# Eight of 24 attention batches: heads in two halves of the array, a new order of beats, four homes for the stacks

## The reference, cut to what matters

```python
q = (x @ Wq + bq).reshape(B, N, 16, 8)
k = (y @ Wk + bk).reshape(B, M, 16, 8)
v = (y @ Wv + bv).reshape(B, M, 16, 8)
attn = softmax(einsum('bnhd,bmhd->bhnm', q, k) / sqrt(8))
out = einsum('bhnm,bmhd->bnhd', attn, v)
h = relu(out @ W1 + b1) @ W2 + b2
```

## Time and profile before

| what | value |
|---|---|
| median of 3 runs | 785.37 us (782.15 to 787.21) |
| profiled execution, first to last instruction | 779.4 us |
| PE busy | 638.1 us (82%), 4712 matmuls |
| DVE busy | 490.8 us (63%) |
| ACT busy | 386.3 us (50%) |
| POOL busy | 302.9 us (39%) |
| stack DMAs from `qk_parts` | 168, of 128 KB each |

### The profile page before, as it was taken

One profiled execution on the slowest core, in us unless ns is written; L12 is line 12 of the kernel. 1 busy time (PEld: TensorE's weight loads), 2 busy tenths in 40 slices (PEclk: granted clock), 3 DMA queues, 4 the chain that ended last, 5 costly groups with the idle time before them and its releaser, 6 DMA issues.

```text
span 779.4 us, 15312 instructions
## 1 busy us (share of the span) xinstructions
PE 638.1 (82%) x4712; PEld 467.2 (60%) x4712; DVE 490.8 (63%) x1428; ACT 386.3 (50%) x860; POOL 302.9 (39%) x456
## 2 busy tenths in 40 slices
PE   2688788889999887899977777748898777699997
PEld 1355666556665544899944555437796566456665
DVE  4678666877778753556867785636657665455443
ACT  5356465466666565466624655335776444232221
POOL 4435355443333036162747644372545730000000
PEclk9999999999999999699976998777999999699999
DMA  6263423333333200144354441012455100223331
GB/s 185 60 158 97 112 73 90 90 94 88 90 95 89 78 19 38 53 130 119 103 138 114 120 128 42 16 41 83 126 143 157 51 11 1 70 69 105 98 95 56
DMA packets 93575, 68.71 MB, mean 88 GB/s; under 512 B 9800, under 2 KB 84424, under 8 KB 93272
## 3 DMA queue, kind: packets, MB, share of 16 engines
q1 hardware_dynamic: 89400, 59.34, 27.4%
q0 software_dynamic: 4096, 8.40, 3.5%
HBM read 30.94 MB, written 14.35 MB: 58 GB/s over the span
## 4 chain that ended last, share of the span: by engine, by line
PE 36%; DVE 8%; issue 6%; DMA 4%; POOL 3%; ACT 3%; SPq 1%; ACTq 0%; DVEq 0%; POOLq 0%
PE ps L2396 7%; PE ps L2406 4%; PE ps L2434 4%; PE ps L2436 4%; PE ps L2447 4%; DVE negmax L975 2%; DMA late<-outputs_moe,placed 2%; PE ps L2111 1%; PE ps L2095 1%; PE ps L2035 1%; PE ps L2390 1%; PE ps L2083 1%; PE ps L2289 1%; POOL gathered L1600 1%; DVE x_sb L1295 1%
## 5 line engine op out<-in xcount | busy, mean ns | idle before, releaser
L975 DVE TENSOR_REDUCE negmax<-ps 128x2 f32<-128x512 f32 x256 | 169.7, 686 | 87.5 <-PE ps L2083 86.8
L1743 ACT ACTIVATE exps<-ps 128x512 f32<-128x512 f32 x256 | 148.6, 598 | 100.7 <-PE ps L2095 99.9
L2083 PE MATMUL ps<-stack 96*128 96x256 bf16 x512 | 102.8, 295 | 26.7 <-DVE negmax L975 23.4
L2095 PE MATMUL ps<-stack 99*128 99x256 bf16 x512 | 100.8, 287 | 19.2 <-DMA stack<-maxt 17.7
L1600 POOL DMA_INDIRECT gathered<-z,placed x64 | 62.4, 975 | 63.3 <-PE ps L2390 28.6
L1618 POOL DMA_INDIRECT late<-outputs_moe,placed x64 | 62.1, 971 | 50.8 <-issue 15.8
L2095 PEld LDWEIGHTS ps<-stack 99*128 99x128 bf16 x512 | 44.2, 102 | 60.2 <-DMA stack<-maxt 24.4
L2083 PEld LDWEIGHTS ps<-stack 96*128 96x128 bf16 x512 | 47.9, 103 | 51.5 <-DVE negmax L975 39.4
L2111 PE MATMUL ps<-exps,values 128*32 128x256 f32 x1024 | 71.9, 398 | 1.3 <-ACT exps L1743 1.0
L1984 ACT ACTIVATE gated<-ps 128x512 f32<-128x512 f32 x36 | 21.5, 597 | 83.1 <-PE ps L2436 83.1
L2406 PE MATMUL ps<-pack_moe,ht 128*128 x368 | 60.1, 288 | 1.3 <-ACT ht L1970 0.8
(11 more groups left out here) (225 smaller groups left out, 1257.4 us busy)
## 6 DMA issues: line engine op xcount, KB each, us to landing
stack<-qk_parts SPq DMA_DIRECT2D x168, 128.0 KB
stack<-weights_t SPq DMA_DIRECT2D x32, 256.0 KB, 3.3
outputs_moe<-y_kept SPq DMA_DIRECT2D x92, 64.0 KB
ht<-gathered SPq DMA_DIRECT2D x44, 128.0 KB, 2.2
pack_moe<-in_moe SPq DMA_DIRECT2D x11, 256.5 KB, 3.9
pack_moe<-in_moe SPq DMA_DIRECT2D x6, 429.5 KB, 4.1
gathered<-y_kept SPq DMA_DIRECT2D x10, 256.0 KB, 3.6
pack_moe<-in_moe SPq DMA_DIRECT2D x1, 1732.0 KB, 7.4
```

The source lines that it names most:

```text
L975: dve.tensor_reduce(negmax_of[b % 2][:, :, h:h + 1].rearrange("p t h -> p (t h)"), ps[:, h % 2, :].rearrange("p (t k) -> p t k", t=2), AX, ...
L1743: nc.scalar.activation(exps[:, i, :], ps[:, 2 + h % 2, :], ACT.Exp, scale=scale)\
L2083: last = pe.matmul(ps[:, h % 2, t * T:(t + 1) * T], st[0:MAXROW, h, 0, t * P:(t + 1) * P], st[0:MAXROW, h, 1, :], start=True, stop=True)
L2095: last = pe.matmul(ps[:, 2 + h % 2, t * T:(t + 1) * T], st[0:MAXROW + 3, h, 1, t * P:(t + 1) * P], st[0:MAXROW + 3, h, 0, :], start=True, ...
```

## The change

`att1` keeps 6 of the 9 pairs, which makes 48 partitions a head (51 with the maxima). Even heads lie in partitions 0 to 50, odd heads in 64 to 114, two heads beside each other at one place of the free axis, so that a batch takes 8 places of a stack tile. The free halves of the three tiles give four homes (`home`). In a beat in which both a column and a row of `att1` are due, one head is even and the other odd, and their four matmuls are issued alternately (`rows_beside_columns`). Columns begin in beat 8 instead of 6, averages are issued in two halves in beats 4j+14 and 4j+15, and the chain, the values, the bias, the mixing and `moe1`'s preparation get other beats. A tail step without work of a batch has 16 beats now. SP issues two DMAs for each pair (one for each half) and two for the maxima; the maxima of the batch that is about to have its columns go between the first pair and the others. The POOL memsets of padding are gone; ACT writes ones instead.

```diff
-    "att1": [(0, 0), (0, 1), (1, 0), (1, 1), (0, 2), (2, 0), (1, 2), (2, 1), (2, 2)],
+    "att1": [(0, 0), (0, 1), (1, 0), (1, 1), (0, 2), (2, 0)],
-MAXROW = 96
+MAXROW = {"att0": 96, "att1": 48, "att2": 96}
+HALF = P // 2
+HALVES = {"att0": 1, "att1": 2, "att2": 1}
-    "moe1": {"stats": ((-1, 3), (2, 3)), "rstd": ((-1, 4), (2, 4)), "norm": ((-1, 8), (2, 6)),
-             "turn": ((-1, 10), (-1, 12), (2, 13), (2, 15)), "turned": ((-1, 11), (-1, 13), (3, 0), (3, 1)),
-             "logits": (-1, 15), "top": (0, 1), "pick": (0, 4), "mark": (0, 6), "exp": (0, 7), "rank": (0, 8),
-             "place": (0, 9), "weigh": (1, 12), "load": (2, 6), "logits2": (3, 3)},
+    "moe1": {"stats": ((-1, 11), (2, 11)), "rstd": ((-1, 12), (2, 12)), "norm": ((-1, 14), (2, 15)),
+             "turn": ((-1, 15), (0, 2), (3, 2), (3, 3)), "turned": ((0, 0), (0, 3), (3, 3), (3, 4)),
+             "logits": (0, 5), "top": (0, 6), "pick": (0, 7), "mark": (0, 9), "exp": (0, 10), "rank": (0, 11),
+             "place": (0, 12), "weigh": (1, 12), "load": (2, 6), "logits2": (3, 6)},
-SEND_FROM = {"moe1": 12, "moe2": 7}
+SEND_FROM = {"moe1": 14, "moe2": 7}
-COL_BEAT = {8: 3, 16: 6}
-GROUP_LAG = 5
-VALUE_BEAT = 4
+COL_BEAT = {8: 3, 16: 8}
+GROUP_LAG = {8: 5, 16: 6}
+GROUP_BEATS = {8: 1, 16: 2}
+VALUE_BEAT = {8: 4, 16: 12}
-PLACE_BEAT = {8: 5, 16: 7}
-MIX_BEATS = {"stats": (5, 5), "rstd": (6, 6), "norm": (7, 10), "turn": (3, 5), "turned": (4, 6), "rk": (6, 10), "gate": (7, 11),
-             "gated": (5, 6), "mixed": (6, 7)}
-CHAIN = ("turn", "finish", "turn_o", "ot", "proj", "hid", "proj2", "residual")
-CHAIN_BEATS = {8: (1, 2, 4, 5, 6, None, None, 7), 16: (1, 2, 4, 5, 6, 7, 9, 10)}
+PLACE_BEAT = {8: 5, 16: 13}
+ROOT_BEAT = {8: 0, 16: 4}
+BIAS_BEAT = {8: 3, 16: 11}
+HOMES = 4
+MIX_BEATS = {"stats": (5, 5), "rstd": (6, 6), "norm": (7, 10), "turn": (3, 7), "turned": (4, 8), "rk": (6, 10), "gate": (7, 11),
+             "gated": (5, 9), "mixed": (6, 10)}
+CHAIN = ("turn", "finish", "turn_o", "ot", "proj", "proj_b", "hid", "proj2", "proj2_b", "residual")
+CHAIN_BEATS = {8: (1, 2, 4, 5, 6, None, None, None, None, 7), 16: (1, 2, 5, 5, 8, 9, 10, 12, 13, 14)}
...
+        def home(s, b):
+            if s == "att1":
+                return 3 + b % HOMES, stack[min(b % HOMES, 2)], 8 * (b % HOMES < 3)
+            return buf(s, b), stack[buf(s, b)], 0
...
-                heads = max([H[s] for s, b in (m, a, d) if valid(b)], default=8)
+                heads = max([H[s] for s, b in (m, a, d) if valid(b)], default=H[stages[-1]] if g > last else 8)
...
+            def spread_slot(s, p, j):
+                nh, dh, (i, st, first), n = H[s], D // H[s], home(s, p), len(SLOTS[s])
+                qa, kc = SLOTS[s][j]
+                for half in range(HALVES[s]):
+                    at = half * HALF + j
+                    sp.dma_start(st[at:at + n * (dh - 1) + 1:n, first:first + nh // HALVES[s], :, :],
+                                 qk_parts[half::HALVES[s], qa:3 + kc + 1:3 + kc - qa, :]).then_inc(stack_in[i], 16)
...
+                    if spreads and sm == "att1":
+                        spread_first(s, p)
+                    if valid(a):
+                        place_maxima(sa, a)
+                    if spreads:
+                        spread_rest(s, p) if sm == "att1" else spread_heads(s, p)
...
-            def fill_rows(i):
-                rows = stack[i][64:MAXROW, 8:16, :, :].rearrange("p h a t -> p (h a t)").bitcast(F32)
-                nc.scalar.activation(rows, zt[64:MAXROW, 0, 0:1].to_broadcast([MAXROW - 64, 8 * T]), ACT.Copy)\
-                    .then_inc(rows_filled, 1)
+            def fill_rows(p):
+                if p == HOMES - 1:
+                    wait(act, "cols_psum", "att0", B - 1)
+                _, st, first = home("att1", p)
+                write_ones(slice(32, HALF), st, first)
+                write_ones(slice(32 + HALF, P), st, first).then_inc(rows_filled, 1)
+                if (s, p, u) == ("att1", 2, 10):
+                    fill_rows(HOMES - 1)
+                    if j == 5:
+                        wait(act, "cols_psum", "att1", B - 1)
+                        fill_ones(2)
...
+            def row_half(s, m, h, t):
+                (at, k), (_, st, first) = half_place(s, h), home(s, m)
+                st = st[at:at + MAXROW[s], first + k, :, :]
+                return pe.matmul(ps[:, h % 2, t * T:(t + 1) * T], st[:, 0, t * P:(t + 1) * P], st[:, 1, :], start=True, stop=True)
+            def rows_beside_columns(s, a, h, m, g):
+                wait_columns(s, a, h)
+                wait_rows(s, m, g)
+                for t in range(2):
+                    column = column_half(s, a, h, t)
+                    row = row_half(s, m, g, t)
+                column.then_inc(sem["cols_psum"], 1)
+                row.then_inc(sem["rows_psum"], 1)
...
                 for st, b, j in due(flow, step, u, "a", group_beats):
-                    averages(st, b, j)
+                    averages(st, b, j, range(3 - GROUP_BEATS[H[st]]))
+                for st, b, j in due(flow, step, u, "a", later_halves):
+                    averages(st, b, j, (1,))
```

More of the change, by code:

```diff
@@ L389, in lists_of @@
         def lists_of(s):
-            return stack[buf("att" + s[3:], B - 3)]
+            return home("att" + s[3:], B - 3)[1]
         picks16 = sb("picks16", [P, len(PART[0]), E], BF16)
@@ L517, in beats @@
                 k = CHAIN_BEATS[H[s]][CHAIN.index(link)]
-                return [] if k is None or (s != "att1" and link in ("hid", "proj2")) else [region_beats(s)[-1] + k - H[s]]
+                return [] if k is None else [region_beats(s)[-1] + k - H[s]]
             return beats
@@ L764, in spread_heads, with place_maxima @@
                         wait(sp, "qk2_ready", s, p)
-                    n = len(SLOTS[s])
-                    sp.dma_start(stack[i][j:j + n * (dh - 1) + 1:n, 0:nh, :, :],
-                                 qk_parts[:, qa:3 + kc + 1:3 + kc - qa, :]).then_inc(stack_in[i], 16)
+                    spread_slot(s, p, j)
+            def spread_heads(s, p):
+                spread_first(s, p)
+                spread_rest(s, p)
+            def place_maxima(s, m):
+                wait(sp, "maxt_ready", s, m)
+                wait(sp, "cols_psum", s, freed(s, m))
+                i, st, first = home(s, m)
+                for half in range(HALVES[s]):
+                    at = half * HALF + MAXROW[s]
+                    sp.dma_start(st[at:at + 3, first:first + H[s] // HALVES[s], 0, :], maxt[half:3 * H[s]:HALVES[s], :])\
+                        .then_inc(maxrow_in[i], 16)
             for flow in FLOWS:
@@ new lines, in wait_columns, with column_half @@
+            def wait_columns(s, a, h):
+                if h == 0:
+                    pe.wait_ge(maxrow_in[home(s, a)[0]], maxrow_total(s, a))
+                    pe.wait_ge(maxrow_ones, min(a + 1, 3) if s == "att0" else 3 if s == "att1" else 4)
+                wait(pe, "exp_ready", s, a, h - 2)
+            def column_half(s, a, h, t):
+                (at, k), (_, st, first) = half_place(s, h), home(s, a)
+                st = st[at:at + MAXROW[s] + 3, first + k, :, :]
+                return pe.matmul(ps[:, 2 + h % 2, t * T:(t + 1) * T], st[:, 1, t * P:(t + 1) * P], st[:, 0, :], start=True, stop=True)
@@ L2109, in averages @@
+                for kt in halves:
                     for k in range(GROUP):
@@ L2126, in turn_max, with find_hidden, find_output @@
                 last.then_inc(sem["maxt_psum"], 1)
+            def find_hidden(s, c):
+                return pe.matmul(ps[:, TURN, c * T:(c + 1) * T], par(s, "w1")[:, c * P:(c + 1) * P], ot[:, :], start=True, stop=True)
+            def find_output(s, t):
+                for c in range(2):
+                    last = pe.matmul(ps[:, ND, (2 + t) * D:(3 + t) * D], hid[:, c, t * P:(t + 1) * P],
+                                     par(s, "w2")[:, c * P:(c + 1) * P], start=(c == 0), stop=(c == 1))
+                return last
             def turn_averages(s, d):
@@ L2159, in beat @@
                     wait(pe, "qk_ready", s, p)
+                    wait(pe, "hid_ready", sd, d - 1) if sd == "att1" and valid(d - 1) else None
                 if u == mix_at("turn", heads) and f2 is not None:
@@ L2204, in beat @@
                 for st, b, _ in due(flow, step, u, "d", chain("proj2")):
[L2205 to L2211 removed]
+                    wait(pe, "hid_ready", st, b)
+                    find_output(st, 0)
+                for st, b, _ in due(flow, step, u, "d", chain("proj2_b")):
+                    find_output(st, 1).then_inc(sem["proj_psum"], 1)
                 for st, b, _ in due(flow, step, u, "m", max_chain("turn")):
[L2213 removed]
+                    if u < VALUE_BEAT[heads]:
                         wait(pe, "v_ready", sm, m)
```

159 lines of the change are left out of this document (78 added, 81 removed).

## The result

The changed kernel takes 791.57 us (median of 5 runs, 789.69 to 791.97) against 785.37 before (a median of 5 as well): 1.0068 times as long, 95% interval 1.0043 to 1.0093. My forecast was 775.2, faster; the time went the other way. The profiled execution has a span of 787.9 us against 779.4, 8.5 us more. In nearly all executions the time is 1.8 us above the span, so the profiled execution of before, at 779.4, lies some 4 us under its median and that of the changed kernel some 2 under its own; about 2 of the 8.5 us are of that kind. Some executions run about 2% longer at a lower granted clock: ratios leave them out while medians don't, so that a median can stand above what its ratio says, and two experiments were profiled in such an execution, so that of those (marked *) only the seam and the steady steps are read.

The account below looks back on a forecast made before the run. PE was taken to bound att1's steps, with DVE next. Terms -23.1 + 17.2 - 11.0 + 1.0 + 1.0 + 1.7 + 3.0 = -10.2 us took 785.4 to 775.2 us; range 764 to 795.

Parts of the forecast that it names:

- Rows beside columns: att1's 105 paired beats: row and column matmuls overlap fully, 0.22 us a beat instead of 0.44; 23.1 us less PE time.
- The first rival: Paired beats of att1: the halves don't run side by side, slower, 798.3 us; chance 0.20, partial overlap included.
- Changes of shape: PE in att1's steps: 19 changes at 0.09 us and four more averages blocks, 2.6 us a step; +17.2 us.
- the second rival: att1's steps: a change between halves and whole array is free, 8 us less, 767 us; chance 0.17.
- The waits: PE from 150 to 300 us: 11 of 11.8 us waiting for maxima, turned output and averages' copy go.
- Crowding of DVE: moe1's first-part statistics, norm and router move by 6 to 8 beats, crowding the step from 264.9; +1 us.
- The end: Behind att1's last columns: router matmuls delay the second projection (+1.7 us), transposes the projection (+1.3 us); +3.0 us.
- Padding and ones: Three POOL memsets go, ACT writes two half-length pieces and extra fills in att1 and moe1; +1 us.
- Four homes: att1's stacks: pairs no longer wait for columns of three batches before; costed at nothing.
- the third rival: att1's steps: waits take other names, from slow DVE beats or SP's issues; 9 of 11 us return, 784 us; chance 0.23.

Follow-up runs that it names:

- seam: The changed kernel, but SP issues the maxima's DMA ahead of the pairs in the step with att1 rows and att0 columns; 780.76 us, ratio 0.992.
- seam_spread: As seam, with statistics and norm of moe1's first 8 tiles in two parts (tiles 0-5 earlier); 779.63 us, ratio 0.9898 to the kernel before.
- seam_unsplit: As seam, with the averages issued again as one block of 16 matmuls in one beat; 785.58 us, ratio 0.9992 to the kernel before.

## Why the prediction was wrong

*Rows beside columns: right.* Column and row mostly start 3 to 7 ns apart, and the four matmuls take the time of two. The first rival (798.3 us) is out, though the time lies near it. The steady steps were forecast as 17.6, 17.6, 16 and 16, 67.2 us together; they take 17.1, 19.0, 16.8 and 15.5, 68.4.

*Changes of shape: too cheap.* I took 0.09 us each way. Entering costs 0.09; leaving costs 0.16 (after four transposes) to 0.22 us (after the values), and part of that is in the first float32 record behind the change. The Trainium skill, TensorEngine Tiling (Array Packing), section Key Properties, says that a change of mode drains the engine, and here the trace agrees for row halves as well. With 9 or 10 excursions a step, 0.07 to 0.13 more each is 0.6 to 1.3 us a step. That the changes are free, the second rival, is wrong. But the runs show that the price is not the lever I took it for: with four blocks fewer in a step PE had less to do and the time did not fall.

*The waits: right in the middle, wrong at its edges, and here is the first of two steps that failed.* I wrote that of SP's issues 1.5 us go before the maxima and that they are hidden as long as a step lasts over 15 us. I worked that out for a step of `att1` alone. In the step where its rows meet `att0`'s columns these begin in beat 3, not 8, and SP's first pair waits for `qk` on top, from 128.15, when the maxima were there, to 130.40. That wait in front of the maxima, with the half clock that came with it, is the +7.9 us, shown by the run that changes the order alone (-8.5 in that step).

*Crowding of DVE: mis-sized and in the wrong step, the second that failed.* I took +1 us for moving `moe1`'s first part, in the step from 264.9. But statistics and norm fall into the step before it, where DVE went from 16.26 to 18.67 us, while it went from 15.87 to 14.82 in the one I named. It cost 2.8 us of waits in one step (1.2 for the maxima, 1.6 for z), and the clock with them: the stretch came out 8.2 us above the forecast, and the norm in two parts with a filled wait brings 5.8 back (64.4 to 58.6). The other 2.4 us stay open; the price of the changes of shape may be part of them, which was not tried there. I counted DVE's work against its free time over a step (18.67 us of 23.2) and not what stands behind one block of 2 us in it.

*The clock: not in the forecast at all.* I read full clock in every window of `att1` and took it as given. The waits of 1.7, 2.0 and 4.0 us that I followed came with 10, 10 and 14 us at half clock, the first of them once with 3.4. But the kernel before waited up to 1.7 us, eight times, for the maxima and kept full clock: which wait costs the clock, the runs don't tell. Nor did every fall stand behind a wait: that of the changed kernel at 271.4 us, 13.7 us long, has PE busy for all of the 5 us ahead of it.

*The end: right.* Forecast +3.0, measured +4.1 in the changed kernel and +2.3 with the seam's order, where the end has 3.4 us at half clock instead of 9.0; moving the two causes back won 2.4 us. *Padding and ones:* the fills take a tenth longer than half, and their +1 us was not tried. The stretch behind the last residual, 1.7 us longer, takes 65.9 to 67.4 us in kernels here that don't differ in it, so that it isn't shown to be of the change. *Four homes: right to cost at nothing,* and some 31 us to lose without it (811.73 against seam's 780.76).

*Waits under other names*, the third rival, came nearest in kind: DVE's maxima stand where the DMA stood. Its price, 784 us, missed the seam.

## What to carry to other kernels

When the order on a queue is changed for the steady step, walk through each step at the border of two phases by itself: the due times there are those of the older phase. Before work is moved to relieve an engine, look at the longest uninterrupted block it makes on its own engine and who waits behind that, not at the sum. And when PE is the bound and made faster, keep it fed: a wait at the wrong place can cost the clock, and even useless matmuls in that wait can be worth more than they take.

## What the runs showed of the hardware

- Matmuls of the two row halves mostly start 3 to 7 ns apart (at most 21 ns in the steady steps), even when both of one half are issued before both of the other.
- Between a pair in halves and full-width or strip work PE loses 0.09 us on entering and 0.14 to 0.22 on leaving.
- The granted clock fell to half within or behind waits of 1.7 to 4.0 us, and 18 transposes in one such wait put the fall off by 10 us (from 16.0 to 26.4 us behind batch 7's `qk`). The Trainium skill, TensorE: Matmul & The Clock Gate, section What's actually happening, says that the gate is set by how busy the engine has been recently; this run agrees. Other falls do not fit it so simply. In the kernel before, PE is busy 3.65 and 2.95 us of each 5 from 146 to 156 us and keeps full clock, while seam's PE is busy 3.62 of the 5 us up to 148.7 and its clock then falls to half, until 162.4. And three falls came with no wait ahead of them, just behind the 16 router matmuls of 8 columns (1.85 us): at 271.4 in the changed kernel, at 264.8 in seam and at 260.1 with the 18 transposes; the same 16 left the clock at full in the kernel before, at 261.53, and in seam_spread, at 256.62. Why stays open. What the fall at 148.7 costs was not tried; an estimate is some 5 us of its step, since it takes 19.4 us with 13.7 at half in seam and 18.2 with 10.2 in seam_unsplit.
